# A graph network kernel: turned one-hots of the attention passes made by ScalarE, and another order at the end of a batch on VectorE

## Chip, cores and metric

One core of one Trainium2 chip runs the whole kernel. The metric is device time in microseconds; the time before is 7100.49 us, the median of 3 runs (7100.11 to 7103.28).

## What is computed

A graph with 6250 nodes of 256 features and 106250 edges sorted by destination goes through four layers, each followed by a residual sum and a layer norm. The reference, cut down:

```python
x = layernorm(x + L0(x))   # x @ W, weighted sum over edges, batch norm, tanh
x = layernorm(x + L1(x))   # 8-head attention over the edges:
                           #   sim = <q[dst], k[src]>; softmax over the edges of one dst; sum of attn * v[src]
x = layernorm(x + L2(x))   # two GAT layers (4 heads, then 1):
                           #   e = leaky_relu(es[src] + ed[dst]); softmax over the edges of one dst; sum of alpha * h[src]
x = layernorm(x + L3(x))   # x @ W.T, degree-normed sum over edges, batch norm, relu, + x
```

## The kernel before

The edges are laid out in tiles of 128, padded so that no tile crosses a block of 128 destination nodes; 16 tiles are a group, and there are 55 groups, 880 tiles. The kernel makes five passes over all tiles, L = 0 to 4. Passes 0 and 4 are plain sums (layers L0 and L3). Pass 1 is the 8-head attention, pass 2 the 4-head GAT layer, pass 3 the 1-head one. Behind each pass comes a node stage over 49 blocks (projections, norms). The passes are divided by barriers of all engines.

In every pass GpSimd issues one indirect gather (line 685) for each tile: 128 rows of a table in HBM, by source node, into a ring of slots in SBUF. Before each four it waits until TensorE has used up what the slots held. TensorE sums a tile into its block of destinations with one product (line 929): the tile's one-hot `ohc` (edge by destination) times the gathered rows, into one of four PSUM banks. VectorE adds the bank to the accumulator `acc` (`add_window`, line 1367); TensorE may be at most four tiles ahead of these adds.

An attention pass works in batches: 16 tiles in pass 1 (55 batches), 32 tiles in passes 2 and 3 (28 batches each). In one turn of the loop the scores of batch b are made and batch b-1 is summed. The turned one-hots `turned[L][par]` are the transposed ones: partition p, edge e is 1 where the edge's destination in its block is p. TensorE uses them to spread a destination's query over its edges (`dest_rows`, line 987, pass 1) or its score term (`dest_scores`, line 974, passes 2 and 3). They have 2048 columns of bf16 in pass 1, 4096 in passes 2 and 3, and two buffers by parity of the batch. They are made from `relb`, the batch's destinations copied to all partitions, which SyncE loads (`rel_row`, line 460) in the middle of its part of the batch before, once the semaphore `oht` says that the one-hots of that batch are made, as there is one buffer for it.

Before the change VectorE makes them: `hot_turned` (line 1406) waits for the load and compares `relb` with the partition's number (line 1409). It is called for batch 0 ahead of the loop, and for batch b+1 near the end of batch b.

The order on VectorE in a batch of pass 1 (`batch`, from line 1533) is written out by hand: eight products of queries and keys (`pair`, line 1429) and their reductions (`dots`, line 1419), with the 16 adds of the batch before and four weightings (`weigh`, line 1509) between them; then a drain and the signal `s` at line 1610, on which TensorE turns the scores (line 1018); then two scans for the segment maxima (`ch1`, lines 1456 and 1459); TensorE's next products (lines 1028 to 1030) gather them into rows; `ch2` (from line 1476) and `ch3` (from line 1494) finish the maxima. In passes 2 and 3 the scores are made at once by `scores_of` (lines 1443 to 1448) and `ch1` to `ch3` stand between adds.

ScalarE's part of a batch (`chain`, from line 750): in passes 1 and 2 it makes the one-hots `ohc` of batch b-1 in groups of four tiles (`hot_four`, lines 744 and 747), by |x - p| and one minus that, clipped at zero; group g waits until TensorE has summed the tiles whose buffers it overwrites. Then it waits for `oht`, copies the first column of the turned one-hots (lines 761 and 762), waits for `ch3`, takes the exponentials (lines 765 and 766), waits for TensorE to turn them back (`pb`) and copies the weights into the ring (lines 771 and 773). In pass 3 VectorE makes `ohc`, and ScalarE ends with weighting the 32 gathered rows (line 780).

Of the kernel before, what the change touches and what calls it, by code (L numbers as in the profile page):

```python
# [7 lines left out]
ALU = mybir.AluOpType  # L8
ACT = mybir.ActivationFunctionType
# [10 lines left out]
NBS = [-(-NB * G // n) for n in GS]  # L20
# [53 lines left out]
def past(L):  # L74

    return sum(NBS[1:L])
# [70 lines left out]
def gnn_kernel(nc, a, out):  # L147
    ctx = ExitStack()
    with ctx:
# [30 lines left out]
        oht = sb("oht", [128, 2, G * 128], BF16)  # L180
# [14 lines left out]
        onesm = sb("onesm", [128, 128])  # L195
# [6 lines left out]
        iota_p = sb("iota_p", [128, 1])  # L202
# [20 lines left out]
        turned = [None] + [[oht[:, 0, :], oht[:, 1, :]]] + 2 * [[oht[:, :, :].rearrange("p u w -> p (u w)"), oht1]]  # L223
        relb = [None, relx[:, :].bitcast(BF16)] + 2 * [aux[:, 2048:4096].bitcast(BF16)]
# [107 lines left out]
        for L in range(5):  # L332
            p = {"agg": sem(f"agg{L}"), **shared_sems}
# [10 lines left out]
            if L in (2, 3):  # L344
                p = {**PASS[L - 1], **p}
# [41 lines left out]
        def tiles_of(L, b):  # L387

            return TS[L] - b * GS[L] if isinstance(b, int) and b == NBS[L] - 1 else GS[L]
# [326 lines left out]
        def _(act):  # L716
            barrier(act)
            for L in range(5):
                p, H, G = PASS[L], HEADS[L], GS[L]
                R = G * H  # L720
                q = NODE[L]
                if L in (0, 1, 4):
                    for m in range({0: 3, 1: 1, 4: 1}[L]):
                        act.wait_ge(q["wt"], m + 1)
                        dst_v = {0: wproj[:, :, 256 * m:256 * m + 256], 1: wout, 4: wout}[L]
                        scale = float(1.0 / (32.0 ** 0.5)) if (L == 0 and m == 2) else 1.0
                        act.activation(dst_v, banks[2 + m % 2][:, :].rearrange("p (k f) -> p k f", k=2), ACT.Copy,
                                       scale=scale).then_inc(q["wc"], 1)
                    if L == 0:
                        act.wait_ge(q["wl"], loaded(L))  # L730
                        act.activation(b3r[L][0:96, 512:768], b3r[L][0:96, 512:768], ACT.Copy,
                                       scale=float(1.0 / (32.0 ** 0.5))).then_inc(q["wc"], 1)
                if H:
                    if L == 1:
                        act.sem_inc(p["w"], 2)
                    rg = rings[L]
                    po_ = VALS[L] + 256

                    def hot_four(c, g):

                        act.wait_ge(p["agg"], c * G + (4 * g + 4 - OHS + 16 * AHEAD[L]))
                        at_k = 4 * g % OHS
                        for j in range(4):
                            act.activation(ohc[:, at_k + j, :], iota[:, :], ACT.Abs, scale=-1.0,  # L744
                                           bias=rel_c[:, ds(c * G + 4 * g + j, 1)])
                        act.drain()
                        act.activation(ohc[:, at_k:at_k + 4, :], ohc[:, at_k:at_k + 4, :], ACT.Relu, scale=-1.0,  # L747
                                       bias=onesm[:, 0:1]).then_inc(p["oc"], 1)

                    def chain(i, o, scores, sums):  # L750
                        b, rset, _, par, _ = batch_at(L, i, o)
                        c, _, _, _, _ = batch_at(L, i, o - 1)
                        if sums and L < 3:
                            for g in range(tiles_of(L, c) // 4):
                                hot_four(c, g)
                        if not scores:
                            return
                        n = tiles_of(L, b)
                        R = n * H
                        act.wait_ge(p["oht"], b + (past(L) + 1))  # L760
                        act.activation(first_in[:, par, 0:1], turned[L][par][:, 0:1], ACT.Copy)
                        act.activation(first_in[:, par, 1:2], turned[L][par][:, 0:1], ACT.Identity, scale=-1.0,
                                       bias=onesm[:, 0:1])
                        act.wait_ge(p["ch3"], b + (past(L) + 1))
                        act.activation(cl[0:R, 3:4], cl[0:R, 2:3], ACT.Exp)  # L765
                        act.activation(px[0:R, :], dd[0:R, :], ACT.Exp)
                        act.drain()
                        act.activation(csel[0:R, 0:H], selh[0:R, n // 32, 0:H], ACT.Copy, scale=cl[0:R, 3:4])\
                            .then_inc(p["px"], 1)
                        act.wait_ge(p["pb"], b + (past(L) + 1))  # L770
                        act.activation(rg[:, rset * G:rset * G + n, po_:po_ + H],
                                       m0[:, 128:128 + R].rearrange("p (h t) -> p t h", h=H), ACT.Copy)
                        act.activation(corr[:, par, 0:H], m1[:, 272:272 + H], ACT.Identity, scale=first_in[:, par, 0:1],
                                       bias=first_in[:, par, 1:2]).then_inc(p["w"], 1)
                        if L == 3:

                            act.drain()
                            for k in range(n):
                                row = rg[:, rset * G + k, 0:256]
                                ins = act.activation(row, row, ACT.Copy, scale=rg[:, rset * G + k, 256:257])  # L780
                                if k % 4 == 3:
                                    ins.then_inc(p["rows"], 1)
                    softmax_batches(act, L, chain)
                barrier(act)
                if L in (0, 4):
                    zT = lambda c, oc: acc[:, c * CHUNK * AW + oc * wide(c):c * CHUNK * AW + (oc + 1) * wide(c)]
                    wide = lambda c: 128 * min(CHUNK, NT - c * CHUNK)
                    for s in range(NCH + 1):
                        if s < NCH:
                            c, w = s, wide(s)  # L790
# [4 lines left out]
                        if s >= 1:  # L795
                            c, w = s - 1, wide(s - 1)
# [19 lines left out]
                for s in range(NT + 12):  # L816
# [13 lines left out]
                    if n is not None and L > 2:  # L830
                        act.wait_ge(q["nm"], through("nm", L) + n + 1)
                        act.activation(X49[:, n, :], X49[:, n, :], ACT.Identity, scale=lnst[:, n % 16, 10:11],
                                       bias=lnst[:, n % 16, 11:12]).then_inc(q["xn"], 1)
# [334 lines left out]
        def _(dve):  # L1168
            v = nc.vector
# [136 lines left out]
            for L in range(5):  # L1306
                p, H, G = PASS[L], HEADS[L], GS[L]
# [19 lines left out]
                if L == 0:  # L1327
                    dve.wait_ge(q["wl"], loaded(L))
                    for j in range(8):
                        kc, pp = j // 4, 32 * (j % 4)  # L1330
                        for i8 in range(8):
                            c = OCT_IDX[i8][j]
# [56 lines left out]
                else:  # L1389
# [13 lines left out]
                        dve.drain()  # L1403
                        tt(part(2), part(1), upper(part(1)), ALU.subtract).then_inc(p["es"], 1)

                    def hot_turned(b, par):

                        dve.wait_ge(p["rx"], b * 16 + (16 * past(L) + 16))
                        v.tensor_scalar(turned[L][par], relb[L], iota_p[:, 0:1], None, ALU.is_equal)\
                            .then_inc(p["oht"], 1)  # L1410

                    def ready(rset, use, k):
                        slot = rset * G + k
                        dve.wait_ge(s_ring[slot // 4], use * 64 + (64 + ring_base(L, slot // 4)))
# [113 lines left out]
                            tt(dens, dens, cw, ALU.mult)  # L1528
                        dve.drain()

                    hot_turned(0, 0)

                    def batch(i, o, scores, sums):
                        b, rset, use, par, ub = batch_at(L, i, o)
                        c, cset, _, cp, _ = batch_at(L, i, o - 1)
                        feed = scores and (not isinstance(b, int) or b + 1 < NBS[L])

                        def add(k0, k1):
                            if sums:
                                for k in range(k0, k1):  # L1540
                                    add_window(c, cp if L == 1 else k // 16, k)
# [30 lines left out]
                        if L == 1:  # L1572
# [30 lines left out]
                            dots(6)  # L1603
                            add(9, 10)
                            pair(7)
                            add(10, 11)
                            dots(7)
                            add(11, 12)
                            if scores:
                                dve.drain()  # L1610
                                dve.sem_inc(p["s"], 1)
                            if feed:
                                hot_turned(b + 1, (o + 1) % 2)
                            if scores:
                                ch1(b, par, ub)
                            add(12, 14)
# [5 lines left out]
                        elif sums and short(L, c):  # L1622
                            begin_sums(c, window_at(0, 0), cp)
                            prepare_four(0)
                            prepare_four(1)
                            add_and_prepare(0, 2)
                            add_and_prepare(1, 3)
                            add(8, 16)
                        else:
                            if sums:  # L1630
                                begin_sums(c, window_at(0, 0), cp)
                            prepare_four(0)
                            if sums:
                                load_offsets(c, 1, 16)
                            prepare_four(1)
                            add_and_prepare(0, 2)
                            add_and_prepare(1, 3)
                            add_and_prepare(2, 4)
                            add_and_prepare(3, 5)
                            if scores:  # L1640
                                scores_of(b, rset, use, par)
                            prepare_four(6)
                            if scores:
                                load_offsets(b, 0, 0)
                                ch1(b, par, ub)
                            add(16, 20)
                            prepare_four(7)
                            if scores:
                                ch2(b, par)
                            add(20, 24)  # L1650
                            if scores:
                                ch3(b, par)
                            if feed:
                                hot_turned(b + 1, (o + 1) % 2)
                            add(24, 32)
                    softmax_batches(dve, L, batch)
                barrier(dve)
# [169 lines left out]
```

## Time and profile before

| what | value |
|---|---|
| median of 3 runs | 7100.49 us |
| profiled execution, its own time | 7108.26 us |
| its span | 7106.3 us |
| busy: TensorE, VectorE, GpSimd, ScalarE | 4563.9, 4512.9, 4531.0, 1770.7 us |
| mean granted TensorE clock | 0.762 |
| gathers in the trace (line 685) | 880 in each of the five passes |
| turned one-hots (line 1409) | 55 in pass 1, 28 in pass 2, 28 in pass 3 |

The share of busy time is a mean over stages with different limits: no engine is over 64% of the span, yet in single stages one is near 90%. Idle time of an engine is given with what ended it; "issue" is time in which it waited for nothing that the profile shows. The ends of matmuls are modelled. Instructions of one engine can overlap a little, so two starts can be closer together than the first one's duration.

### The profile page before, as it was taken

The numbers are of one execution on the slowest core, as the hardware profiler recorded it, in microseconds if no ns is written. First come the engines' busy times: TensorE is split into PE (matmuls) and PEld (weight loads), VectorE is DVE, ScalarE is ACT, GpSimd is POOL, SyncE is SP. The second block draws the span as 40 slices with busy tenths as digits, with TensorE's granted clock in tenths as the row PEclk, the third lists the DMA queues.
The fourth block names the chain that finished last, engine by engine and source line by source line (L and its number), as shares of the span: only waits on it lengthen the run. The fifth ranks groups of instructions, "written<-read, shape, count | busy, mean of one in ns | idle before, by whom it ended". The sixth has DMA issues, their size and how long they took to land.

```text
span 7106.3 us, 100710 instructions
## 1 busy us (share of the span) xinstructions
PE 4563.9 (64%) x17172; PEld 3064.9 (43%) x17173; DVE 4512.9 (64%) x11642; ACT 1770.7 (25%) x4933; POOL 4531.0 (64%) x4940
## 2 busy tenths in 40 slices
PE   3555556867777777784666667567667635555556
PEld 1333334444444444463444444344444423433433
DVE  5555555558988988874666666655555564544446
ACT  0000000523333333342344333433333340000004
POOL 5777776145555555516777776377777737777771
PEclk7777777878887887896777777777777767777776
DMA  3333334378888888845444445244444453333334
GB/s 80 105 105 105 105 105 101 108 242 291 288 293 291 290 294 288 283 130 150 129 129 129 128 128 103 89 128 127 127 132 127 125 133 105 104 105 104 105 104 90
DMA packets 499024, 1083.92 MB, mean 153 GB/s; under 512 B 105385, under 2 KB 296492, under 8 KB 491469
## 3 DMA queue, kind: packets, MB, share of 16 engines
q0 software_dynamic: 240064, 696.46, 35.3%
q1 hardware_dynamic: 258603, 384.24, 16.2%
q14 instruction: 320, 2.62, 0.1%
q8 instruction: 37, 0.61, 0.0%
HBM read 1010.63 MB, written 71.05 MB: 152 GB/s over the span
## 4 chain that ended last, share of the span: by engine, by line
PE 32%; POOL 19%; issue 19%; DVE 17%; DVEq 5%; DMA 4%; ACT 2%; POOLq 0%; SPq 0%; ACTq 0%
POOL ring L685 19%; PE bank L929 19%; DVE acc L1367 5%; PE bank L974 3%; DVE aux L1429 2%; DVE ring L1509 2%; PE bank L1156 2%; DMA ring<-g_t,stage 2%; PE bank L987 2%; DVE ohc L1373 1%; PE bank L1109 1%; DVE sc L1419 1%; DVEq L1479 1%; DMA aux<-q_t 1%; DVEq L1367 1%
## 5 line engine op out<-in xcount | busy, mean ns | idle before, releaser
L929 PE MATMUL bank<-ring,ohc 128*128 128x256 f32 (+3 forms) x8800 | 3083.3, 508 | 1366.0 <-DMA ring<-xs_t,stage 403.4
L929 PEld LDWEIGHTS bank<-ring,ohc 128*128 128x128 f32 x8800 | 2080.2, 251 | 2213.2 <-issue 1033.5
L1367 DVE TENSOR_TENSOR acc<-acc,bank 128x256 f32 (+3 forms) x4400 | 1855.2, 422 | 1515.8 <-PE bank L929 1374.1
L685 POOL DMA_INDIRECT ring<-g_t,stage x1760 | 1782.0, 1013 | 522.0 <-issue 470.3
L685 POOL DMA_INDIRECT ring<-kv_t,stage x880 | 863.4, 981 | 665.8 <-PE bank L929 419.5
L685 POOL DMA_INDIRECT ring<-in_x,stage x880 | 837.1, 951 | 274.4 <-issue 257.5
L685 POOL DMA_INDIRECT ring<-xs_t,stage x880 | 836.7, 951 | 261.0 <-issue 258.0
L744 ACT ACTIVATE ohc<-iota,rel_c 128x128 f32<-128x128 f32 x1760 | 558.0, 388 | 238.9 <-PE bank L929 238.7
L793 ACT ACTIVATE aux<-bank 128x512 f32<-128x512 f32 (+1 forms) x26 | 14.9, 572 | 2231.0 <-PE bank L1098 2231.0
L765 ACT ACTIVATE cl<-cl 128x1 f32<-128x1 f32 (+3 forms) x111 | 22.5, 203 | 2186.4 <-DVE mx L1502 2186.4
L1509 DVE TENSOR_TENSOR ring<-ring 128x1024 f32<-128x1024 f32 (+1 forms) x550 | 554.6, 1009 | 9.5
L987 PE MATMUL bank<-aux,oht 128*128 128x256 bf16 x2640 | 445.3, 326 | 150.3 <-DVE aux L1429 111.6
L987 PEld LDWEIGHTS bank<-aux,oht 128*128 128x128 bf16 x2640 | 284.4, 116 | 282.1 <-DVE aux L1429 175.5
L1373 DVE TENSOR_SCALAR ohc<-iota,rel_c,relx 128x128 f32<-128x128 f32 x883 | 321.4, 364 | 87.8 <-issue 86.2
L780 ACT ACTIVATE ring<-ring 128x256 f32<-128x256 f32 x880 | 353.9, 493 | 2.3
L1376 DVE TENSOR_SCALAR ohc<-iota,rel_c 128x128 f32<-128x128 f32 x883 | 271.4, 308 | 97.6 <-issue 97.6
L747 ACT ACTIVATE ohc<-ohc,onesm 128x512 f32<-128x512 f32 x440 | 317.6, 722 | 32.3
L1429 DVE TENSOR_TENSOR aux<-bank,ring 128x512 f32<-128x512 f32 x440 | 300.6, 683 | 33.4 <-PE bank L987 23.2
L1419 DVE TENSOR_REDUCE sc<-aux 128x16 f32<-128x512 f32 x440 | 299.5, 681 | 4.0
L1021 PE MATMUL bank<-ident,sc 128*128 128x128 f32 (+3 forms) x112 | 36.1, 422 | 387.6 <-DVE sc L1448 387.6
L1156 PE MATMUL bank<-wproj,ring 128*128 128x512 f32 (+2 forms) x588 | 211.3, 484 | 26.6 <-ACT ring L850 16.3
L712 POOL MEMSET acc<- 128x264 f32 x98 | 31.2, 318 | 260.6 <-DVE ring L1745 260.6
(274 smaller groups left out, 4058.4 us busy)
## 6 DMA issues: line engine op xcount, KB each, us to landing
aux<-q_t SPq DMA_DIRECT2D x880, 192.0 KB, 5.0
aux<-relb_t SPq DMA_DIRECT2D x56, 1024.0 KB
relx<-relb_t SPq DMA_DIRECT2D x55, 512.0 KB
ring<-g_t,stage POOLq DMA_INDIRECT x1760, 2.8
x<-ring SPq DMA_DIRECT2D x21, 896.0 KB, 4.3
ring<-x SPq DMA_DIRECT2D x21, 896.0 KB, 9.4
mk<-mk SPq DMA_DIRECT2D x445, 32.1 KB
ring<-in_x,stage POOLq DMA_INDIRECT x880, 2.8
```

The source lines that it names most:

```text
L685: g_.indirect_dma_start(out=rings[L][:, slot, 0:W], out_offset=None, in_=table[L][:, :], in_offset=bass.IndirectOffsetOnAxis(ap=stage[:, s ...
L744: act.activation(ohc[:, at_k + j, :], iota[:, :], ACT.Abs, scale=-1.0, bias=rel_c[:, ds(c * G + 4 * g + j, 1)])
L747: act.activation(ohc[:, at_k:at_k + 4, :], ohc[:, at_k:at_k + 4, :], ACT.Relu, scale=-1.0, bias=onesm[:, 0:1]).then_inc(p["oc"], 1)
L780: ins = act.activation(row, row, ACT.Copy, scale=rg[:, rset * G + k, 256:257])
L929: return mm(agp[k % 4][:, 0:width], ohc[:, hot, :], rg[:, slot, vo:vo + width], start=True, stop=True)
L987: ins = mm(qe[r % 2][:, 256 * j:256 * j + 256], oht[:, par, 128 * k:128 * k + 128], qw[:, k % 8, 256 * part:256 * part + 256], start=part ...
L1156: ins = mm(ob[:, 0:w1], xv[:, 128 * k:128 * k + 128], wproj[:, k, 0:w1], start=k == 0, stop=k == 1 and L > 0)
L1367: tt(win, win, agp[k % 4][:, 0:width], ALU.add).then_inc(p["added"], 1)
L1373: ins = v.tensor_scalar(ohc[:, k % 8, :], iota[:, :], rel, ew_c[:, ds(b * G + k, 1)], ALU.is_equal, ALU.mult)
L1419: v.tensor_reduce(sc[:, par, 0:R].rearrange("p (h t) -> p t h", h=H)[:, 2 * r:2 * r + 2, :], prod[:, r % 2, :, :].rearrange("p t (h d) -> ...
L1429: tt(prod[:, r % 2, :, :], qe[r % 2][:, :].rearrange("p (t w) -> p t w", t=2), rg[:, rset * G + 2 * r:rset * G + 2 * r + 2, 0:256], ALU.mu ...
L1509: return tt(vv, vv, wv, ALU.mult)
```

## The change

ScalarE makes the turned one-hots in all three attention passes, in two ACTIVATEs with a drain between them: |p - x|, and one minus that, clipped at zero. The first is called ahead of the loop, the others in `chain` after the first four groups of `ohc` (in pass 3, where ScalarE makes no `ohc`, at its head). ScalarE's wait for `oht` goes away. On VectorE the calls of `hot_turned` go away; in pass 1 the adds of tiles 10 and 11, which stood before and behind the last reduction, come behind the signal `s`.

```diff
+                    def hot_turned(b, par):
+
+                        act.wait_ge(p["rx"], b * 16 + (16 * past(L) + 16))
+                        act.activation(turned[L][par], relb[L], ACT.Abs, scale=-1.0, bias=iota_p[:, 0:1])
+                        act.drain()
+                        act.activation(turned[L][par], turned[L][par], ACT.Relu, scale=-1.0, bias=onesm[:, 0:1])\
+                            .then_inc(p["oht"], 1)
+
+                    hot_turned(0, 0)
+
                     def chain(i, o, scores, sums):
                         b, rset, _, par, _ = batch_at(L, i, o)
                         c, _, _, _, _ = batch_at(L, i, o - 1)
-                        if sums and L < 3:
-                            for g in range(tiles_of(L, c) // 4):
-                                hot_four(c, g)
+                        feed = scores and (not isinstance(b, int) or b + 1 < NBS[L])
+                        hots = tiles_of(L, c) // 4 if sums and L < 3 else 0
+                        for g in range(min(hots, 4)):
+                            hot_four(c, g)
+                        if feed:
+                            hot_turned(b + 1, (o + 1) % 2)
+                        for g in range(4, hots):
+                            hot_four(c, g)
                         if not scores:
                             return
                         n = tiles_of(L, b)
                         R = n * H
-                        act.wait_ge(p["oht"], b + (past(L) + 1))
...
-                    def hot_turned(b, par):
-
-                        dve.wait_ge(p["rx"], b * 16 + (16 * past(L) + 16))
-                        v.tensor_scalar(turned[L][par], relb[L], iota_p[:, 0:1], None, ALU.is_equal)\
-                            .then_inc(p["oht"], 1)
...
-                    hot_turned(0, 0)
...
                             pair(7)
-                            add(10, 11)
                             dots(7)
-                            add(11, 12)
                             if scores:
                                 dve.drain()
                                 dve.sem_inc(p["s"], 1)
-                            if feed:
-                                hot_turned(b + 1, (o + 1) % 2)
+                            add(10, 12)
                             if scores:
                                 ch1(b, par, ub)
...
                             if scores:
                                 ch3(b, par)
-                            if feed:
-                                hot_turned(b + 1, (o + 1) % 2)
                             add(24, 32)
```

## Rows read from the trace of the kernel before

**Rows 1.** Stages: pass 1, 2 and 3; window, its length, busy time by engine.

```profile
core 0: us, PE busy (x) PEld busy (x) DVE busy (x) ACT busy (x) POOL busy (x), PEclk, DMA share, GB/s
1600.00:3000.00 1400.00, 1014.37 (x4706) 676.78 (x4704) 1260.22 (x2604) 455.67 (x1350) 797.20 (x850) 0.81 0.88 291
3300.00:4350.00 1050.00, 723.58 (x2718) 495.45 (x2719) 699.79 (x1517) 411.22 (x1128) 821.49 (x822) 0.74 0.46 129
4660.00:5650.00 990.00, 684.22 (x2683) 460.08 (x2684) 554.37 (x1468) 340.34 (x929) 764.39 (x811) 0.74 0.45 129
```

**Rows 2.** Groups on GpSimd in passes 1, 2, 3, 4: busy, mean ns, idle before.

```profile
L685 POOL DMA_INDIRECT ring<-kv_t,stage x800 | 785.5, 982 | 600.6 <-PE bank L929 381.7 <-issue 218.9
...
L685 POOL DMA_INDIRECT ring<-g_t,stage x773 | 802.6, 1038 | 228.7 <-issue 203.1 <-PE bank L929 25.6
...
L685 POOL DMA_INDIRECT ring<-g_t,stage x763 | 754.8, 989 | 225.8 <-issue 203.5 <-PE bank L929 22.2
...
L685 POOL DMA_INDIRECT ring<-xs_t,stage x826 | 785.4, 951 | 244.4 <-issue 242.3 <-PE bank L929 2.2
```

**Rows 3.** Line 1409 on VectorE: min/median/max ns, first and last start.

```profile
L1409 DVE TENSOR_SCALAR oht<-relx,iota_p x55: 752/753/755, 1513.2 to 3030.0; 128x2048 bf16<-128x2048 bf16 x55
L1409 DVE TENSOR_SCALAR oht<-aux,iota_p x28: 1265/1278/1433, 3231.1 to 5655.0; 128x4096 bf16<-128x4096 bf16 x28
```

**Rows 4.** Timeline, gathers beside line 1409, passes 2 and 3: start us, us.

```profile
3836.58 1.82 POOL L685 DMA_INDIRECT ring<-g_t,stage  x1 [0.30 <-issue]
...
3837.00 1.28 DVE L1409 TENSOR_SCALAR oht<-aux,iota_p 128x4096 bf16<-128x4096 bf16 x1
...
3881.49 1.68 POOL L685 DMA_INDIRECT ring<-g_t,stage  x1 [0.30 <-issue]
...
4906.33 1.55 POOL L685 DMA_INDIRECT ring<-g_t,stage  x1 [0.30 <-issue]
...
5071.89 1.79 POOL L685 DMA_INDIRECT ring<-g_t,stage  x1 [0.30 <-issue]
```

**Rows 5.** Timeline, the end of one batch of pass 1 and the next start.

```profile
2209.64 0.68 DVE L1429 TENSOR_TENSOR aux<-bank,ring 128x512 f32<-128x512 f32 x1
...
2211.17 0.41 DVE L1367 TENSOR_TENSOR acc<-acc,bank 128x264 f32 x1
...
2211.78 0.45 PE L1018 MATMUL bank<-ident,sc 128*128 128x128 f32 x1 [3.69 <-DVEq L1610]
...
2215.61 0.27 DVE L1476 TENSOR_TENSOR rows<-bank,cneg_r 1x120 f32<-1x120 f32 x1 [0.73 <-PE bank L1030]
...
2220.34 0.69 DVE L1429 TENSOR_TENSOR aux<-bank,ring 128x512 f32<-128x512 f32 x1 [0.41 <-issue]
...
2221.07 0.69 DVE L1419 TENSOR_REDUCE sc<-aux 128x16 f32<-128x512 f32 x1
```

**Rows 6.** Pass 1: line 1018 in three batches; two windows behind it, granted clock.

```profile
1904.68 0.45 PE L1018 MATMUL bank<-ident,sc 128*128 128x128 f32 x1 [3.67 <-DVEq L1610]
1932.15 0.45 PE L1018 MATMUL bank<-ident,sc 128*128 128x128 f32 x1 [3.67 <-DVEq L1610]
1960.52 0.45 PE L1018 MATMUL bank<-ident,sc 128*128 128x128 f32 x1 [3.67 <-DVEq L1610]
...
1960.50:1964.50 4.00, 3.98 (x12) 1.84 (x12) 2.42 (x5) 0.00 (x0) 2.83 (x3) 0.50 1.03 385
1988.60:1992.50 3.90, 3.74 (x13) 1.71 (x14) 2.69 (x7) 0.00 (x0) 2.78 (x3) 0.64 1.05 386
```

**Rows 7.** The page's groups: ScalarE's ACTIVATEs at 128 and 512 columns.

```profile
L744 ACT ACTIVATE ohc<-iota,rel_c 128x128 f32<-128x128 f32 x1760 | 558.0, 388 | 238.9 <-PE bank L929 238.7
...
L747 ACT ACTIVATE ohc<-ohc,onesm 128x512 f32<-128x512 f32 x440 | 317.6, 722 | 32.3
```

**Rows 8.** Waits in pass 1 (1600 to 3000): in total, times, longest.

```profile
ACT cl L765 <- DVE mx L1502: 880.4, 50, 18.1
```

**Rows 9.** Timeline, pass 2: ScalarE's fifth group, and TensorE behind the turned scores.

```profile
3813.93 1.28 ACT L744 ACTIVATE ohc<-iota,rel_c 128x128 f32<-128x128 f32 x4 [7.76 <-PE bank L929]
...
3826.49 3.41 PE L929 MATMUL bank<-ring,ohc 128*128 128x261 f32 x8
```

More of the change, by code:

```diff
@@ L1535, in batch @@
                         c, cset, _, cp, _ = batch_at(L, i, o - 1)
-                        feed = scores and (not isinstance(b, int) or b + 1 < NBS[L])
                         def add(k0, k1):
```

## The prediction, made before the result was known

> **What bounds the kernel now.** I read the stages first: busy time by engine in the steady part of the three attention passes. VectorE is busy 1260 of 1400 us in pass 1, 90%; in passes 2 and 3 it has 67% and 56%, and GpSimd is the fullest engine with 78% and 77% [rows 1]. Then I read what GpSimd does between its gathers [rows 2]. In passes 2 and 3 its idle time is 229 and 226 us for 773 and 763 gathers, 0.30 us each, nearly all "issue"; that is its own gap, the same 0.30 us as in pass 4. It never waits long for another engine there, so **passes 2 and 3 last as long as GpSimd's row of gathers**. In pass 1 it waits 382 us for TensorE, so something else sets that pass: VectorE's batch, with a stretch in which it waits for TensorE.
>
> One more thing is to be seen in [rows 2]: a gather takes 951 ns in pass 4, but 1038 and 989 ns in passes 2 and 3. The timeline shows one cause [rows 4]. Where VectorE makes the turned one-hots (L1409, 128x4096 bf16), the gather beside it takes 1.82 or 1.68 us in pass 2 and 1.55 or 1.79 us in pass 3.
>
> **The change, part by part.** VectorE loses L1409: 55 of 753 ns in pass 1, and 28 of 1.28 us into one buffer (as many into the other) in passes 2 and 3 together [rows 3]. ScalarE gets two ACTIVATEs for each.
>
> *ScalarE's new work.* No row shows an ACTIVATE this wide. 128 columns take 388 ns and 512 take 722 ns [rows 7]: 0.87 ns a column, so 2.06 us at 2048 and 3.84 us at 4096; a batch costs 4.1 us in pass 1 and 7.7 us in passes 2 and 3. From below the slope cannot be bounded better than by these rows; even at half of it the argument stands. Is there room? In pass 1 ScalarE waits 880 us in 50 batches, 17.6 us each, for VectorE's last softmax step [rows 8]; 4.1 us fit. In pass 2 the pair stands after the fourth group of one-hots, where ScalarE waits 7.76 us today before the fifth, which TensorE needs 12.6 us after its start, and which takes some 2 us [rows 9]: 7.7 us fit into the wait, and some 10 us more could be late. In pass 3 ScalarE is busy 340 of 990 us, some 14 of 41 us a batch. So I cost it at nothing on the path; without that cover it would be 4.1 or 7.7 us a batch.
>
> [...]
>
> *Pass 1, the end of a batch.* Today the order is product 7 (2209.64), an add, its reduction, an add (2211.17 to 2211.58), then the signal to TensorE, which turns the scores at 2211.78 [rows 5]. After the change the reduction follows the product at once. Such a pair shows 0.73 us from start to start (2220.34, 2221.07), so it ends at 2209.64 + 0.73 + 0.68 = 2211.05, and the signal comes 0.53 us earlier. From the turned scores to VectorE's next stage at 2215.61 it is TensorE's matmuls that count, 3.83 us; the two adds moved behind the signal (0.34 us apart) take the place of L1409 under them and change nothing there. So the batch shortens by 0.53 us, not by the 0.75 us of L1409: the rest becomes more waiting for TensorE. 54 batches have both halves: **-28.6 us**. [...] A loss in this part needs a wait that is not there today. [...]
>
> *Passes 2 and 3, the gathers.* Without L1409 beside it a gather is back to 0.95 us: 0.87 and 0.73 us less in pass 2, where the two kinds alternate, mean 0.80; 0.60 or 0.84 us in pass 3, where I count two of the first to one of the other, mean 0.68 [rows 4]. As GpSimd sets the length, each counts in full: 28 x 0.80 = 22.4 us and 28 x 0.68 = 19.0 us, **-41.4 us**. Bounds: nothing, if the gather meets another slow neighbour instead; the full 1.28 us each, 72 us, if more than the lengthened gather hides in it. VectorE's own 1.28 us less and its place count nothing here. In pass 1 the same effect is small and on an engine that waits.
>
> [...]
>
> *Starts and waits.* The first one-hots of each pass come from ScalarE too, at worst 3.4 us later in pass 1 and 6.4 us in 2 and 3. In passes 2 and 3 the first scores wait for 32 gathers of 1.25 us, 40 us, so nothing shows; in pass 1 up to 3.4 us. I take zero. The wait for ScalarE's copy of the one-hots' first column goes away and costs nothing. SyncE loads the next row of destinations after the one-hots of this batch; these come earlier in every pass, so that load does too. ScalarE now waits for that row with its exponentials queued behind.
>
> **Sum.** 28.6 + 41.4 = 70.0 us. The profiled execution took 7108.3 us: 7038.3. It stands 7.8 us above the median of the runs, so 7030.5.
>
> **The rivals.**
> [...]
> *B, the gathers keep their time* because another neighbour takes the place: 7100.5 - 28.6 = 7072. Against: each of the four rows has its cause beside it.
> *C, slower: ScalarE stuck before its exponentials.* In pass 1 it takes up the one-hots right after the four groups, 17.6 us before VectorE hands it the maxima. If the row of destinations for the next batch landed later than 17.6 - 4.1 = 13.5 us after that, TensorE's turn back and the weights would be late in all 54 batches. From 70 / 54 = 1.3 us beyond that point the kernel is slower; at 3 us beyond it is 7100.5 - 70 + 162 = 7192. Against: the load is ordered before the batch begins, and nothing waits for it today.
> *D, the change is not what it says*, its ACTIVATEs being as hidden as VectorE's L1409: no change, 7100. Against: L1409 is on the busiest engine.
>
> **Chances.** My forecast 0.62; A long 0.12; A short 0.11; B 0.06; C 0.05; D 0.04. The range must hold 8 in 10: from 7002, A short with a little more from the gathers, to 7066, which takes in A long with some 7 us less from the gathers; outside lie B, C, D. A measurement of this kernel can tell some 0.2%, 14 us. Faster by more: forecast, A and B, 0.91; the same: D, 0.04; slower: C, 0.05.
>
> **What would show it.** Right: gathers in passes 2 and 3 at means near 1011 and 967 ns with idle time still 0.30 us each; pass 1's batches near 27.4 us, TensorE's wait before the turned scores 3.1 instead of 3.69 us; ScalarE's wait before its exponentials shorter by 4 us and still over 10. Wrong: a wait of ScalarE for the row of destinations, TensorE waiting for ScalarE's one-hots, GpSimd waiting for TensorE in passes 2 or 3, or gathers that are long beside the new ACTIVATEs.

## The result: 2.0% slower, and the profile after

The changed kernel takes 7242.07 us (median of 4 runs, 7235.94 to 7249.77) beside 7100.3 us for the kernel before: ratio 1.0201, interval 1.0189 to 1.0214. The forecast was 7030.5 us, and 7242 lies far outside its range, on the other side. The profiled execution took 7249.77 us, its span 7247.9 against 7106.3.

First the stages, as in [rows 1]: window and length in us, busy time by engine, TensorE's granted clock, DMA share, GB/s.

```profile
1600.00:3000.00 1400.00, 917.70 (x4145) 608.49 (x4143) 1079.49 (x2245) 576.15 (x1289) 708.50 (x752) 0.75 0.77 257
3300.00:4350.00 1050.00, 711.50 (x2900) 498.03 (x2898) 648.26 (x1537) 578.34 (x1245) 752.76 (x790) 0.76 0.48 137
4660.00:5650.00 990.00, 667.82 (x2708) 451.92 (x2708) 529.90 (x1529) 535.22 (x1105) 715.87 (x809) 0.74 0.45 130
```

The windows are those of [rows 1]. Passes 2 and 3 begin later now (first gathers at 3398.5 and 4730.6 us), so the second and third row hold some 100 and 70 us of what goes before; only the first compares like with like. In pass 1 everything has become thinner: VectorE is busy 1079 us instead of 1260 and has got through 2245 instructions instead of 2604. The engine that set the pass stands still more, and does less.

The length of pass 1 can be read from its 55 turned scores on TensorE (first and last start). The first row is of the kernel before, the second of the changed one.

```profile
L1018 PE MATMUL bank<-ident,sc x55: 299/444/448, 1541.3 to 3061.7; 128*128 128x128 f32 x55
```

```profile
L1032 PE MATMUL bank<-ident,sc x55: 299/306/448, 1537.2 to 3242.7; 128*128 128x128 f32 x55
```

1520.4 us have become 1705.5: **pass 1 has lost 185 us**. From first gather to last, pass 2 went from 1193.3 to 1181.5 us, pass 3 from 1143.3 to 1114.2 and pass 4 from 1109.0 to 1105.8: 44 us gained. 185 - 44 = 141, the whole difference. The 3 us of pass 4, which the change doesn't touch, come with its gathers: their median is 946 ns instead of 949, in every pass. Why is open.

Now the waits of pass 1 (1600 to 3000 us: in total, times, longest), where [rows 8] had one row:

```profile
ACT cl L779 <- DVE mx L1510: 781.1, 45, 22.6
...
PE bank L1001 <- DVE aux L1437: 246.6, 120, 8.8
...
DVE aux L1437 <- issue: 188.5, 22, 9.6
...
PE bank L1032 <- DVEq L1613: 137.7, 44, 3.2
```

The third row is new. VectorE stands 188.5 us in 22 stops, 8.6 us each, with no engine and no transfer named. TensorE's wait on VectorE's product (second row) is the same stop seen from its consumer. The timeline shows one (start us, us, engine, line; in brackets the idle time before):

```profile
2227.45 0.30 PE L1032 MATMUL bank<-ident,sc 128*128 128x128 f32 x1 [3.12 <-DVEq L1613]
...
2231.46 0.27 DVE L1484 TENSOR_TENSOR rows<-bank,cneg_r 1x120 f32<-1x120 f32 x1 [0.92 <-PE bank L1044]
...
2235.80 0.29 DVE L1510 TENSOR_TENSOR mx<-bank,mx 128x128 f32<-128x128 f32 x1
2236.13 0.20 ACT L779 ACTIVATE cl<-cl 128x1 f32<-128x1 f32 x1 [13.27 <-DVE mx L1510]
2244.79 0.69 DVE L1437 TENSOR_TENSOR aux<-bank,ring 128x512 f32<-128x512 f32 x1 [8.70 <-issue]
2245.52 0.69 DVE L1427 TENSOR_REDUCE sc<-aux 128x16 f32<-128x512 f32 x1
2245.62 1.67 PE L1001 MATMUL bank<-aux,oht 128*128 128x256 bf16 x7 [8.15 <-DVE aux L1437]
```

L1510 is the last step of a batch's softmax, L1437 the first product of the next batch. One batch earlier the same pair (L1510 at 2208.28, L1437 at 2208.61) had nothing between. VectorE's loop holds two batches, and the stop is in every second one: it stands **at the jump back to the head of the loop**. Batches alternate between 27.32 and 36.04 us. Between jumps they are as short as forecast.

That points at the loading of code. The page's row for the queue that brings instructions (packets, MB, share) is, before and after:

```profile
q14 instruction: 320, 2.62, 0.1%
```

```profile
q14 instruction: 458, 3.75, 0.2%
```

138 loads more, of 8 KB each (3.75 MB / 458): 124 of them in the loop of pass 1, 12 in that of pass 4. In the kernel before, none falls into the steady part of pass 1 (between 1603.8 and 3010.2 us). Here are the loads of one round of the loop in the changed kernel, from the records of that queue, with the number of the loop's instruction that VectorE had begun last, counted from 1 (0: none since the jump):

```
load at, us   2208.8  2234.7 | 2239.5  2242.7  2245.2
instruction   139     264    | 0       1       4         (jump back at 2235.9)
```

In this round the two loads in straight code come 125 instructions apart; in 24 rounds of the loop it is 123 to 138, 129.6 in the mean. I take one load, one block of code, to be 128 instructions: an estimate from these distances, which the runs below test. After the jump three loads come one by one, 3.2 and 2.5 us apart here (5.0 and 2.5 us in the median of the 25 jumps), while VectorE begins four instructions. The stop of 8.6 us is in fact two: VectorE's own records, those of its sequencer included, have the jump at 2235.90, the loop's first instruction at 2241.34 and its second at 2244.57. The place of VectorE's pass-1 loop in the built programs differs by two instructions: it began at its instruction 1475 and had 276; now it begins at 1473 and has 272. The two that have gone ahead of it are those of the first `hot_turned` of pass 1. The second stop stands between instructions 1473 and 1474. If a block of 128 begins at 1474, the old loop touched three blocks and the new one, shorter, touches four: 1 + 128 + 128 + 15. **Theory P, the place of the code:** three blocks stay loaded over the jump, four don't. **Rival W, the work:** the stop comes from what the change does (the order of the adds, ScalarE's new work, transfers behind it).

### The profile page after: what moved, and what is told of

The parts are those of the page before. It is cut to its first block, busy times and chain, and to the rows that moved or that the text cites. A ratio compares the mean times of both kernels' runs of the same rounds, so it can differ in the third digit from the quotient of the medians.

```text
span 7247.9 us, 100880 instructions
## 1 busy us (share of the span) xinstructions
PE 4567.9 (63%) x17172; PEld 3060.1 (42%) x17173; DVE 4412.4 (61%) x11531; ACT 2389.1 (33%) x5155; POOL 4490.1 (62%) x4940
## 3 DMA queue, kind: packets, MB, share of 16 engines
q14 instruction: 458, 3.75, 0.2%
## 4 chain that ended last, share of the span: by engine, by line
PE 31%; issue 20%; POOL 19%; DVE 17%; DVEq 5%; DMA 4%; ACT 2%; SPq 0%; POOLq 0%; ACTq 0%
POOL ring L685 18%; PE bank L943 18%; DVE acc L1381 5%; PE bank L988 3%; DVE aux L1437 3%; DMA ring<-g_t,stage 2%; DVE ring L1517 2%; PE bank L1170 2%; DVE sc L1427 1%; PE bank L1123 1%; DVE ohc L1387 1%; PE bank L1001 1%; DMA aux<-q_t 1%; DVEq L1381 1%; DVEq L1487 1%
## 5 line engine op out<-in xcount | busy, mean ns | idle before, releaser
L685 POOL DMA_INDIRECT ring<-g_t,stage x1760 | 1742.8, 990 | 521.7 <-issue 467.0
L1437 DVE TENSOR_TENSOR aux<-bank,ring 128x512 f32<-128x512 f32 x440 | 301.1, 684 | 240.4 <-issue 220.9
L755 ACT ACTIVATE oht<-oht,onesm 128x2048 bf16<-128x2048 bf16 (+1 forms) x83 | 213.9, 2578 | 5.7
```

The lines of the kernel that those rows point to most:

```text
L685: g_.indirect_dma_start(out=rings[L][:, slot, 0:W], out_offset=None, in_=table[L][:, :], in_offset=bass.IndirectOffsetOnAxis(ap=stage[:, s ...
L1437: tt(prod[:, r % 2, :, :], qe[r % 2][:, :].rearrange("p (t w) -> p t w", t=2), rg[:, rset * G + 2 * r:rset * G + 2 * r + 2, 0:256], ALU.mu ...
```

## The experiments

**1 to 4: the place alone.** Instructions that compute nothing, on VectorE, ahead of the pass-1 loop. Nothing in the loop changes.

```diff
                 if L == 1:
+                    for k in range(8):      # 120 in the second and fourth
+                        v.memset(fw[0:1, k:k + 1], 0.0)
                     dve.wait_ge(q["wl"], loaded(L))
```

e1_after_8_first, the changed kernel with 8 (the loop begins at 1481):

> The changed kernel with 8 one-element memsets on VectorE ahead of the loop of pass 1, in a stretch where VectorE waits some 10 us for loads. Theory 1 (where VectorE's code lies): in the changed kernel every second batch of pass 1 starts 8 to 9 us late with VectorE waiting for nothing that the trace names, while blocks of code are loaded, because its loop starts two instructions earlier than before; 8 instructions more move it back, the waits go, pass 1 falls from 1727 to about 1515 us between its first and last gather, and the kernel takes 7025 to 7045 us. Theory 2 (ScalarE's new work, the load of the next row or the moved adds make the wait): nothing changes, 7240 us.

e2_before_120_first, the kernel before with 120 (1595):

> The kernel before, unchanged but for 120 one-element memsets on VectorE ahead of the loop of pass 1. Theory 1 (where VectorE's code lies): its loop of 276 instructions then runs over four blocks of 128 instead of three, every second batch waits 3 to 9 us for code, and the kernel takes 7180 to 7350 us. Theory 2 (the new work makes the wait): 7100 us, with at most some 5 us for the memsets.

e3_before_8_first, the kernel before with 8 (1483):

> The kernel before with 8 one-element memsets at that place. Both theories: 7100 us within 5; a loop moved by 8 instructions still lies in three blocks by theory 1. It tells what the memsets cost by themselves.

e4_after_120_first, the changed kernel with 120 (1593):

> The changed kernel with 120 memsets. Theory 1: the loop of 272 instructions starts 10 instructions before the end of a block and runs over four blocks again, so code is loaded at each jump back and the kernel takes 7100 to 7260 us. If the waits are gone as with 8, not the count of blocks but something else about the place decides: 7035 us. Theory 2: 7240 us.

Beside 7117.58 us for the kernel before: **e1 7043.03 us, ratio 0.9897 (0.9881 to 0.9914); e2 7289.25 us, 1.0244 (1.0227 to 1.0262)**; e3 7110.44 and e4 7215.89 us in one run each. Eight empty instructions turn the changed kernel from 2% slower into 1% faster, and 120 of them make the old kernel, which has nothing of the change, 2.4% slower. The turned scores of the four:

```profile
L1032 PE MATMUL bank<-ident,sc x55: 299/447/449, 1543.7 to 3031.6; 128*128 128x128 f32 x55
```

```profile
L1018 PE MATMUL bank<-ident,sc x55: 299/446/448, 1542.7 to 3238.7; 128*128 128x128 f32 x55
```

```profile
L1018 PE MATMUL bank<-ident,sc x55: 300/382/448, 1545.3 to 3062.9; 128*128 128x128 f32 x55
```

```profile
L1032 PE MATMUL bank<-ident,sc x55: 299/303/448, 1548.0 to 3211.7; 128*128 128x128 f32 x55
```

Set beside the place of the loop:

```
kernel           loop begins  instr.  blocks  55 turned scores   code loads   in the first block
before               1475      276      3        1520.4 us           320           127
before + 8           1483      276      3        1517.6              321           119
before + 120         1595      276      4        1696.0              446             7
after                1473      272      4        1705.5              458             1
after + 8            1481      272      3        1487.9              321           121
after + 120          1593      272      4        1663.7              447             9
```

The fourth column decides whether the stops are there, in both kernels, whatever the work. W is excluded as their cause. Beside the same kernel with its loop in three blocks the three slow placements lose 217.6 us (after), 178.4 (e2) and 175.8 (e4). In e2 the stops stand in the old kernel's waits of pass 1, 5.8 us at most, and e4 has 118.1 us in 32 on the same instruction:

```profile
DVE aux L1431 <- issue: 158.1, 45, 5.8
```

The last column is confirmed by where the second stop falls, in each of the 25 jumps back of pass 1: behind the loop's 1st instruction in the changed kernel, its 7th in e2, its 9th in e4. By the places of the loops that is instruction 1474, 1602 and 1602 of the program, 128 apart, the estimate of a block. One jump of e2:

```profile
2046.83 0.29 DVE L1504 TENSOR_TENSOR mx<-bank,mx 128x128 f32<-128x128 f32 x1
2051.83 0.69 DVE L1431 TENSOR_TENSOR aux<-bank,ring 128x512 f32<-128x512 f32 x1 [4.71 <-issue]
2052.56 0.69 DVE L1421 TENSOR_REDUCE sc<-aux 128x16 f32<-128x512 f32 x1
2056.38 0.69 DVE L1431 TENSOR_TENSOR aux<-bank,ring 128x512 f32<-128x512 f32 x1 [3.14 <-issue]
```

So the first block and the second are waited for one after the other. In the changed kernel only one instruction, without work for the engine, stands between the two waits (medians 3.9 and 4.9 us from start to start); in e2 and e4 a product and a reduction, or two of each, run while the second is on its way, and a jump costs 7 us instead of 8.7.

**5 to 8: the parts, first attempt.** Order alone (e5), move to ScalarE alone (e6), pass 1 alone on ScalarE (e7), passes 2 and 3 alone (e8), all with 8 ahead. The diffs of three stand below; in e7 VectorE keeps passes 2 and 3 as before, and ScalarE has pass 1 alone:

```diff
-                        if feed:
+                        if feed and L in (1,):
                             hot_turned(b + 1, (o + 1) % 2)
```

> Only the new order at the end of a batch; VectorE still makes the turned one-hots, ahead of the two moved adds. 8 memsets keep the loop of pass 1 in three blocks (as in all runs that follow). Theory: the signal for the turned scores comes 0.53 us earlier as in the full change, but VectorE now has L1409 (0.67 us from start to start) and two adds (0.68 us) before the scans, of which TensorE's stretch of 3.83 us hides all but the part that delays TensorE's product behind the scans; a batch takes 27.4 to 27.7 us against 27.94, and the kernel 7085 to 7105 us beside 7117 for the kernel before on this chip. Rival, VectorE's sum alone sets the batch: nothing gained, 7117.

> Only the move to ScalarE, in all three passes, with the old order of the adds on VectorE. Theory: with nothing between the signal and the scans, VectorE waits for TensorE there, which sets that stretch; pass 1 gains 0 to 0.25 us a batch (0 to 14 us), passes 2 and 3 the 41 us of the gathers: 7062 to 7080 beside 7117. Rival, VectorE's busy time sets the batch: 0.75 us a batch more, 7035.

> Move and order in pass 1 alone; passes 2 and 3 as before. Theory: pass 1 gains 0.63 us a batch as in the changed kernel with 8 memsets (27.31 against 27.94), 34 us: 7080 to 7088 beside 7117. Rival, the gain lies in passes 2 and 3 alone: 7117.

> The move in passes 2 and 3 alone; pass 1 as before, order too. Theory: 56 gathers get back 0.60 to 0.87 us each, 41 us: 7073 to 7080 beside 7117, with VectorE's one-hots gone from beside the gathers. Rival, other neighbours take the place: 7105 to 7117, with mean gathers still above 1020 and 980 ns.

While they ran, every kernel took a sixth longer, the one before too, with waits strewn over all engines and passes, so they don't tell what the change is worth at the usual speed. Beside 8267.81 us for the kernel before of the same session:

```
e5   order alone         8267.21 us   0.9998 (0.9987 to 1.0008)
e6   move alone          8334.81      1.0068 (1.0046 to 1.0089)
e7   pass 1 alone        8273.55      1.0001 (0.9981 to 1.0021)
e8   passes 2, 3 alone   8325.93      1.0074 (1.0050 to 1.0099)
```

They do tell that the gain isn't to be had in every condition: the move in passes 2 and 3, worth half a per cent below, made the kernel 0.7% slower there (e8, and e6). What slowed the session, and why the move loses in it, is open. Three were run again, as e9 to e11; pass 1 alone was not, it comes out by difference.

**9 to 11: the parts.** All three have the 8 empty instructions ahead of the loop, which the diffs below don't show. e9_move_alone is the changed kernel with the old order of the adds:

```diff
                             pair(7)
+                            add(10, 11)
                             dots(7)
+                            add(11, 12)
...
-                            add(10, 12)
```

> The same kernel as the move alone, again, since in the four runs before this one every kernel took 8240 to 8340 us, the kernel before too, with waits of 2 to 5 us strewn over all engines. Theory: the move alone gains 0 to 14 us in pass 1 and the 41 us of the gathers in passes 2 and 3: 0.6% to 0.8% under the kernel before. Rival, VectorE's busy time sets the batch of pass 1: 1.1% under it. Second rival, ScalarE's one-hots cost passes 2 and 3 what the gathers give: no difference, or slower.

e10_order_alone is the kernel before with the new order, L1409 still on VectorE, behind the signal:

```diff
                             pair(7)
-                            add(10, 11)
                             dots(7)
-                            add(11, 12)
...
                                 hot_turned(b + 1, (o + 1) % 2)
+                            add(10, 12)
```

> The same kernel as the order alone, again, for the same reason. Theory: batches of pass 1 of 27.4 to 27.7 us against 27.94, 0.2% to 0.4% under the kernel before; passes 2 and 3 unchanged. Rival, VectorE's sum alone sets the batch: no difference.

e11_passes23_alone leaves pass 1 as before and lets ScalarE make the turned one-hots in passes 2 and 3 alone (`if feed and L in (2, 3,):`).

> The same kernel as passes 2 and 3 alone, again, for the same reason. Theory: 41 us less, 0.58% under the kernel before, with the gathers' mean at 1011 ns in pass 2 and 968 in pass 3. Rival, other neighbours take the place: within 0.2% of it.

**12: a loop that reloads today.** Pass 2's loop (376 instructions) lies in four blocks even in e1. e12_pass2_in_three is e1 with 86 more empty instructions ahead of that loop, which put it into three:

```diff
                 if L == 2:
+                    for k in range(86):
+                        v.memset(fw[0:1, k:k + 1], 0.0)
                     dve.wait_ge(q["wl"], loaded(L))
```

> The changed kernel with 8 memsets, and 86 more ahead of the loop of pass 2, whose 376 instructions then fit into three blocks of 128 instead of four. Theory (code waits cost only where VectorE is on the path): VectorE's waits of some 3 us at each jump back in pass 2 go, fewer blocks of code are loaded, but GpSimd's gathers set the pass and the time is that of the changed kernel with 8 memsets, within 5 us (1.03% under the kernel before). Rival (code loads slow the gathers or the pass too): 12 times 3 us, up to 36 us less.

Beside 7101.8 us for the kernel before:

```
e9   move alone          7061.89 us   0.9944 (0.9927 to 0.9961)   -39.9
e10  order alone         7096.04      0.9991 (0.9982 to 1.0001)    -5.8
e11  passes 2, 3 alone   7063.47      0.9947 (0.9930 to 0.9964)   -38.3
e12  all, in three       7035.43      0.9911 (0.9895 to 0.9928)   -66.4
```

*Passes 2 and 3* are worth 38 us by themselves. The gathers of passes 2 and 3 in e11 (busy us, mean ns, idle before):

```profile
L685 POOL DMA_INDIRECT ring<-g_t,stage x699 | 714.3, 1022 | 206.9 <-issue 182.2 <-PE bank L946 24.7
```

```profile
L685 POOL DMA_INDIRECT ring<-g_t,stage x673 | 647.2, 962 | 199.1 <-issue 174.5 <-PE bank L946 24.5
```

Against 1038 and 989 ns [rows 2]: 880 x (16 + 27) ns = 38 us, the whole of it. I had expected 41 us and 1011 and 968 ns; what became of the rest stands with the prediction's terms below. The time of e9, 0.56% under the kernel before, also falls just short of the 0.6 to 0.8% expected.

*Pass 1* is then worth 66.4 - 38.3 = 28 us, but neither half gets it alone: e9 gives 1.6 us beyond e11, and e10 gives 5.8, which its interval doesn't tell from nothing. I had expected 0.2 to 0.4% of e10: a miss. The 55 turned scores of the same session say it more sharply: 1515.3 us in e11, where pass 1 is as before, 1516.0 in e9, 1516.9 in e10 and 1486.1 in e12, which has both. The means over pass 1, in us, show what becomes of each half:

```
                    TensorE's wait   turned scores to   turned scores to   batch
                    before L1018     VectorE's scan     row (L1476)
before                  3.68              0.70               3.85          27.97
e9, move alone          3.67              0.44               3.76          27.92
e10, order alone        3.13              1.60               4.32          27.85
e1, both                3.13              1.14               3.81          27.32
```

The order brings the signal 0.55 us earlier, but with L1409 and both adds ahead of it VectorE's scan starts 0.90 us later behind the turned scores, and the row 0.47 us later: given back. The move takes 0.75 us out of a stretch in which TensorE is awaited anyway; in e9 VectorE waits there instead, where the trace of before has no such row (waits of pass 1, e9):

```profile
DVE fw L1466 <- PE bank L1032: 31.6, 50, 0.7
```

Together the adds take the place of L1409, and the 0.55 us stay: a batch of e1 is 0.65 us shorter.

*Code loads where VectorE isn't awaited.* In pass 2 e1 has the first row below (waits, 3300 to 4350 us), and e12 has none like it; its code loads fall from 321 to 262:

```profile
DVE acc L1537 <- issue: 36.4, 12, 3.3
```

```profile
q14 instruction: 262, 2.15, 0.1%
```

Yet against their own runs of the kernel before e12 gains 66.4 us and e1 74.6 us, with intervals that overlap: the rival's 36 us aren't there. The stops, 3.0 us at each jump of pass 2, cost nothing that these runs can tell while GpSimd sets the length; in pass 1, where VectorE sets it, they cost 217.6 us. My 5 us around e1 was missed, on the slow side, and the traces show a reason: from first to last gather pass 2 takes 1182.2 us in e12 and 1175.7 in e1, as without the stops more gathers fall beside VectorE's adds (112 longer than 1.1 us, 71 in e1). That is one trace each.

**The best version** is the changed kernel with eight empty instructions, 0.9897, or e12, 0.9911; their intervals overlap. Both beat both kernels.

## Why the prediction was wrong

**The step that failed:** "A loss in this part needs a wait that is not there today." There was one, and it needed no engine and no transfer to cause it. I costed the edit by the instructions it removes, adds and moves, and not by where those that stay come to lie. The size of what I left out: 1705.5 us in the changed kernel against 1487.9 with the loop in three blocks, 217.6 us over the 25 jumps back of 26 rounds, 8.7 us each.

**The danger could be seen blind.** The waits of pass 2 (3300 to 4400 us) in the kernel before hold this row, which I took for nothing as GpSimd sets that pass:

```profile
DVE acc L1527 <- issue: 38.5, 12, 3.4
```

It is a stop of 3.2 us at each jump back, in a loop of 380 instructions that touches four blocks. VectorE's pass-1 loop has 276 and no such row. The question to ask was how far its 276 were from a fourth block. The code loads answer it roughly: in straight code they are seen (rounds of pass 1 in the changed kernel, e2 and e4) when the 3rd to the 13th instruction of a block is the last begun, and in the kernel before one came (at 1549.9 us) when the loop's fourth was. So the loop began at most some ten instructions behind a block's start, on the side on which the change takes two away. That two were enough came out only with the changed kernel.

What the runs show of the mechanism: a load brings 8 KB (3.75 MB in 458). The pass-1 loop stayed loaded in three blocks (before, e1 and e3 have no load from the first jump back to the last) and not in four (5 loads a round in the changed kernel). In straight code the loads stopped nobody: in pass 1 of the changed kernel VectorE's waits on "issue" other than those at the jump last 0.4 us at most. At the jump they cost 8.7 us.

Point by point, the rest:

- *Passes 2 and 3*, forecast -41.4 us: measured -40.9 from first to last gather, -38.3 in e11. That the sum fits is luck: 22.4 and 19.0 forecast, 11.8 and 29.1 measured. These are the gathers of the changed kernel, pass 2 and pass 3, against [rows 2]; I had said 1011 (by my own terms 1012) and 967 ns:

```profile
L685 POOL DMA_INDIRECT ring<-g_t,stage x780 | 801.2, 1027 | 230.7 <-issue 207.4 <-PE bank L943 23.3
```

```profile
L685 POOL DMA_INDIRECT ring<-g_t,stage x750 | 717.6, 957 | 221.8 <-issue 196.3 <-PE bank L943 25.5
```

  The price of L1409 was right. Here are all gathers over 1.1 us of the traces before and after, by the VectorE instruction that they lie beside longest: what they take beyond 0.95 us, in us, and their number.

```
                              pass 2             pass 3
beside                    before    after    before    after
turned one-hots (L1409)   21.9 28   none     19.1 28   none
weightings                23.7 45   41.3 71  none      none
adds                      19.8 82   18.1 73   1.0  5    2.2 10
one-hots of tiles         none      none     11.5 34    4.1 13
others                     1.5  7    0.2  1  none      none
```

  In pass 2 much of what L1409 gave back, 17.6 us, went to gathers that now lie beside the weightings: rival B, in large part true there. One of them, with no wide ACTIVATE near:

```profile
3453.58 2.50 DVE L1517 TENSOR_TENSOR ring<-ring 128x1024 f32<-128x1024 f32 x2
...
3454.03 1.59 POOL L685 DMA_INDIRECT ring<-g_t,stage  x1 [0.31 <-issue]
```

  In pass 3 the one-hots of tiles lengthened fewer gathers than before, which I hadn't counted on. My step of counting a shortened gather in full, with the rest of them as they were, was wrong both times. Some 2.6 us a pass of the gain are the 3 ns of each gather that pass 4 has too.

- *Pass 1*, forecast -28.6 us by 0.53 us a batch: where the loop doesn't reload, -28 by difference, and 29.7 us between the turned scores of e3 and e1 (1517.6 and 1487.9). TensorE's wait is 3.1 us as forecast; batches are 27.3 instead of 27.4. Rival A had TensorE's clock or the transfers set pass 1, with every batch of the long kind or every one of the short (28.37 and 27.47 us in [rows 6]), 4 or 53 us; the ends of my range rest on the two. Neither form came, and no run shows what makes a batch long or short: the turning of the scores (L1032) takes 447 ns at the median of e1, near its longest of 449 (299 at best), and yet e1's batches alternate between 27.5 and 27.1 us.
- *ScalarE's work costs nothing*: right. Its two ACTIVATEs in pass 1 (busy us, mean ns), of which [rows 7] had given 2.06 us each at most:

```profile
L755 ACT ACTIVATE oht<-oht,onesm 128x2048 bf16<-128x2048 bf16 x44 | 88.1, 2002 | 3.0
L753 ACT ACTIVATE oht<-relx,iota_p 128x2048 bf16<-128x2048 bf16 x44 | 87.4, 1986 | 0.0
```

  In e1 ScalarE waits 664.2 us in 51 times, 13.0 us each, before its exponentials, 4.6 less than in [rows 8], and in that window never for the row of destinations. Two ACTIVATEs of 2.0 us thus take the place of 0.75 us on VectorE [rows 3], and still e1 has a ratio of 0.9897: VectorE is the busiest engine in pass 1 (90% of the window in [rows 1]) and lengthened gathers in passes 2 and 3 (1.55 to 1.82 us beside L1409 [rows 4]).
- *No long gathers from ScalarE's ACTIVATEs*: right. In passes 2 and 3 of the changed kernel 341 gathers have no instruction of VectorE beside them, 42 of these have such an ACTIVATE, and none of the 341 takes over 0.98 us. A 128x4096 ACTIVATE of the changed kernel and the gathers beside it, pass 2:

```profile
3810.65 3.69 ACT L753 ACTIVATE oht<-aux,iota_p 128x4096 bf16<-128x4096 bf16 x1
```

```profile
3810.62 0.95 POOL L685 DMA_INDIRECT ring<-g_t,stage  x1 [0.30 <-issue]
3811.87 0.94 POOL L685 DMA_INDIRECT ring<-g_t,stage  x1 [0.30 <-issue]
3813.11 0.94 POOL L685 DMA_INDIRECT ring<-g_t,stage  x1 [0.30 <-issue]
```

  Beside L1409 on VectorE a gather took 1.55 to 1.82 us [rows 4].
- *Rival C*, the slower one, had the right sign and the wrong mechanism: in the steady part of pass 1 nothing waits for the row of destinations. Rival D is out, as the parts show.

The sum of the terms, 70.0 us, fits the changed kernel when its pass-1 loop lies in three blocks: e12 gives 66.4 and e1 74.6, with the luck in passes 2 and 3 told above. What was timed was that kernel with its loop in four.

## What to carry to other kernels

Before costing an edit, look in the trace for waits on "issue" at the jump back of each engine's loops, count the loops' instructions, and ask which loop on a critical engine lies close to one block more; then cost any edit ahead of it or in it, even one that only removes instructions. When a kernel gets slower with new "issue" stops at the head of a loop and a higher count of instruction loads, shift the loop by a few empty instructions before judging the idea. And two edits that meet in one stretch between two engines are to be costed together: here either alone was worth next to nothing.

## What was not expected of the hardware

- VectorE's code came in loads of 8 KB (3.75 MB in 458), and the second stops lay 128 instructions of the program apart (1474, 1602). The pass-1 loop in three such blocks ran without a load (before, e1, e3); in four it loaded each round: 5 loads a round, and 8.7 us a jump in the changed kernel's pass 1. Pass 2's loop has 5 loads a round and stops of 3.0 us in e1, and neither in e12. All six placements of the pass-1 loop agree. The changed kernel's pass-4 loop (394 instructions from 4543) lies in five and has 76 loads in 13 rounds, against 64 before, at no cost in time where GpSimd sets the length (1105.8 us against 1109.0).
- The stops were shorter where more work stood in the loop's first block: with 1 instruction in it (the changed kernel) the two waits add up to 8.6 us, with 7 or 9 (e2, e4) a jump costs 7.1 or 7.0 us, and with 82 (pass 2 before) only one wait of 3.2 us is left.
- An instruction of VectorE can lengthen a gather beside it (1.59 us beside a weighting and 1.55 to 1.82 beside L1409, against a median of 0.95), and the length of a GpSimd stage then hangs on which ones fall together: the weightings beside 71 gathers instead of 45 cost pass 2 17.6 us more (41.3 against 23.7).
- With the stops TensorE's granted clock over pass 1 was 0.75, against 0.84 in the same window of e1 and 0.81 before [rows 1]; in the stop of the timeline above (2236.2 to 2244.7) it was 0.60. What this adds to the batches was not separated.
